# One block for the edge loop and the last stage of an edge-gated graph kernel, with the further passes ahead of both

## What is computed

```python
pre_u = einsum('bud,dk->buk', h, W1[:256]);  pre_v = einsum('bvd,dk->bvk', h, W1[256:])
S   = sigmoid(einsum('buvk,ko->buvo', relu(pre_u[:,:,None] + pre_v[:,None] + b1), W2)[...,0] + b2[0])
a_t = einsum('buv,bud->bvd', S * adj, h)
m_t = einsum('uv,bud->bvd', adj, h) * h
out = beta1*h + beta2*(a_t @ Wa + ba) + beta3*(m_t @ Wm + bm)
```

## Time and profile before

| | us |
|---|---|
| median of 3 runs | 3447.57 |
| lowest and highest | 3445.82, 3448.07 |
| the profiled execution, its own time | 3449.29 |
| its span, first to last instruction | 3447.2 |
| PE busy in the span | 3356.6 (97%) |
| DVE, ACT, POOL busy | 2841.7, 2342.5, 1836.9 |

### The profile page before, as it was taken

How to read it: one execution, slowest core, us unless ns; L and a number is a source line. 1 busy time by engine, 2 the same in 40 slices (tenths; PEclk the granted TensorE clock), 3 DMA queues, 4 the chain that set the end, 5 groups by cost and what they waited for, 6 DMA issues and landing times. The chain is left out here.

```text
span 3447.2 us, 56125 instructions
## 1 busy us (share of the span) xinstructions
PE 3356.6 (97%) x14230; PEld 2618.5 (76%) x14230; DVE 2841.7 (82%) x4857; ACT 2342.5 (68%) x14070; POOL 1836.9 (53%) x2379
## 2 busy tenths in 40 slices
PE   7999999999998999999999999999999999689999
PEld 5667667676666888778878888878878888578888
DVE  5566765766547999999999999999999999469897
ACT  1222121221116999899999999999999999688997
POOL 3221221221114667656666676666666665578886
PEclk9999999999999999999999999999999999899999
DMA  7876777767669656775675666666656647587775
GB/s 273 296 262 240 264 255 247 284 248 256 230 205 225 155 122 165 165 171 139 139 174 132 176 137 159 171 152 153 168 141 168 155 114 189 183 285 249 263 257 193
DMA packets 345402, 685.80 MB, mean 199 GB/s; under 512 B 38990, under 2 KB 252856, under 8 KB 323512
## 3 DMA queue, kind: packets, MB, share of 16 engines
q1 hardware_dynamic: 289088, 594.50, 59.6%
q0 software_dynamic: 21504, 53.31, 5.0%
q10 hardware_dynamic: 34480, 34.34, 2.9%
HBM read 444.01 MB, written 256.18 MB: 203 GB/s over the span
## 5 line engine op out<-in xcount | busy, mean ns | idle before, releaser
L1240 ACT ACTIVATE junk<-psum_a 128x128 f32<-128x128 f32 x6144 | 1611.5, 293 | 199.0 <-PE psum_a L1144 110.2
L1240 ACT ACTIVATION_READ_ACCUMULATOR junk<-psum_a 128x1 f32 x6144 | 1367.8, 224 | 0.0
L1185 DVE TENSOR_REDUCE group_sum<-psum_d 128x56 f32<-128x896 f32 x1024 | 1111.5, 1085 | 87.8 <-PE psum_d L1144 42.0
L1144 PE MATMUL psum_d<-v_t,pk 128*128 128x512 f32 x1920 | 754.6, 393 | 0.0
L1292 POOL DMA_INDIRECT sum_dram<-total,idx_all x512 | 506.9, 990 | 228.3 <-POOL total L1303 124.1
L996 POOL TENSOR_TENSOR own<-whole 128x256 f32<-128x256 f32 x128 | 126.0, 985 | 753.9 <-DVE own_mixed L789 420.3
L1143 PE MATMUL psum_d<-u_t,pk 128*128 128x512 f32 x1280 | 503.9, 394 | 5.8 <-issue 4.7
L689 PE MATMUL wide<-shared,h 128*128 128x512 f32 x1024 | 482.2, 593 | 0.0
L747 ACT COPY whole<-ring 128x256 f32<-128x256 f32 x128 | 47.7, 373 | 630.4 <-PE ring L661 630.4
L1144 PE MATMUL psum_a<-v_t,pk 128*128 128x512 f32 x1152 | 453.4, 394 | 0.0
L1604 ACT ACTIVATE masked<-masked,of_u,half_sign 128x128 f32<-128x128 f32 x1024 | 399.7, 480 | 61.7 <-POOL masked L1541 61.7
(11 more groups left out here) (225 smaller groups left out, 5532.8 us busy)
## 6 DMA issues: line engine op xcount, KB each, us to landing
rows_dram<-split SPq DMA_DIRECT2D x128, 512.0 KB, 3.2
sum_dram<-zero SPq DMA_DIRECT2D x128, 512.0 KB, 4.0
u_t<-rows_dram SPq DMA_DIRECT2D x64, 1024.0 KB
shared<-sum_dram SPq DMA_DIRECT2D x64, 1024.0 KB, 6.3
first_u<-rows_dram SPq DMA_DIRECT2D x62, 1024.0 KB
pk<-pick_dram SPq DMA_DIRECT2D x448, 128.0 KB
whole_dram<-whole SPq DMA_DIRECT2D x128, 256.0 KB, 3.4
pick_dram<-first_v SPq DMA_DIRECT2D x128, 256.0 KB, 3.0
```

The source lines that it names most:

```text
L1144: return nc.tensor.matmul(dst, pk[n % PKS][:, SLOTS + at:SLOTS + at + P], part(v_t[n % VG][:], b, LB), start=False, stop=True)
L1185: nc.vector.tensor_reduce(out_[:, :, 1:EG], in_[:, :, GW:LATE].rearrange("p b (g k) -> p b g k", k=GW), AX, ALU.add, apply_absolute_value= ...
L1240: last = nc.scalar.activation(junk[:, a % RING_A, k * LATE:(k + 1) * LATE], psum_a[a % RING_A][:, k * LATE:(k + 1) * LATE], ACT.Abs, accum ...
```

## The change

- `passes_i` is read into registers right behind the first stage, and the branch over the further passes stands there, ahead of the edge loop (before, both stood behind it). A semaphore `passes_made` says that DVE has written the number; SP also waits for all `rows_stored` there, since further passes would read those rows.
- Edge loop and last stage are one block: the functions `edges_sp`, `edges_pe` and so on, each followed by `last_sp`, `last_pe` and so on, on the same engine. The barrier, the reading of the register and the branch between them are gone. In their place PE waits for the last drained sums, and SP and POOL for all scatters.
- The POOL adds of tiles k = 0 and 1 are made inside the edge loop, one half each behind the scatters of cells n = 251 to 254.
- Their outputs `masked0` and `masked1` (`masked_ahead`) take the place of the second `hWa_ahead` tile in `shared`: only `hWa_all[0]` is loaded ahead, and `hWa_all[1]` is the first load of `last_sp`. The adj tiles of k = 0 and 1 are loaded ahead.
- DVE scales `of_u` behind cell 254 in place of behind cell 255.

Lines that only moved or were indented anew are left out; where one is shown for its place it has the old indentation.

```diff
@@ first stage: behind its last work, and behind the block
-                            link(nc.vector.tensor_copy(passes_i[:], most[:, 1:2]))
+                            nc.vector.tensor_copy(passes_i[:], most[:, 1:2]).then_inc(passes_made, 1)
...
+                    for i in range(RW):
+                        sp.wait_ge(rows_stored[i], 32 * ((B * NT - i + RW - 1) // RW))
+                    sp.wait_ge(passes_made, 1)
...
+            passes = nc.values_load(passes_i[0:1, 0:1], min_val=0, max_val=PASSES)
             nc.all_engine_barrier()
...
+        with nc.If(passes > 1):
...
-        hWa_ahead = [shared[:, i * ROW:(i + 1) * ROW].rearrange("p (b d) -> p b d", d=D) for i in range(RAW)]
+        hWa_ahead = shared[:, 0:ROW].rearrange("p (b d) -> p b d", d=D)
+        masked_ahead = [shared[:, ROW + i * P * B:ROW + (i + 1) * P * B].rearrange("p (b v) -> p b v", v=P) for i in range(RAW)]
@@ edge loop, SP at n == AHEAD
                             for t in range(RAW):
                                 sp.dma_start(raw[t], sum_uv[t * P:(t + 1) * P, 0:P, :]).then_inc(raw_loaded[t], 16)
-                                sp.dma_start(hWa_ahead[t], hWa_dram[:, t * P:(t + 1) * P, :].rearrange("b p d -> p b d")).then_inc(hWa_loaded[t], 16)
+                            sp.dma_start(adj_first[t][:], adj[t * P:(t + 1) * P, 0:P]).then_inc(adj_loaded[t], 16)
+                        sp.dma_start(hWa_ahead, hWa_dram[:, 0:P, :].rearrange("b p d -> p b d")).then_inc(hWa_loaded[0], 16)
@@ edge loop, POOL behind the scatters of cell n
+                    if n >= n_blk - 5 and n < n_blk - 1:
+                        k, m = divmod(n - (n_blk - 5), 2)
+                        some = slice(m * HV, (m + 1) * HV)
+                        pool.wait_ge(raw_loaded[k], 16)
+                        pool.wait_ge(of_v_loaded[m], 16)
+                        pool.wait_ge(left_d, LD * LEFT)
+                        pool.wait_ge(left_a, LA * LEFT)
+                        TT(masked_ahead[k][:, :, some].rearrange("p b v -> p v b"), raw[k][:, some, :], of_v[:, some, :],
+                           ALU.add).then_inc(raw_added, 1)
+                for i in range(RING_S):
+                    pool.wait_ge(scattered[i], 16 * TILES * ((n_blk - i + RING_S - 1) // RING_S))
@@ behind the edge loop
-            nc.all_engine_barrier()
-        passes = nc.values_load(passes_i[0:1, 0:1], min_val=0, max_val=PASSES)
-        with nc.If(passes > 1):
...
+            def last_pe(pe):
+                pe.wait_ge(drained_d, ND * n_blk)
+                pe.wait_ge(drained_a, NA * n_blk)
...
-                            if RAW <= k < NT:
+                        if 1 <= k < NT:
...
+                @block.gpsimd
+                def _(pool):
+                    edges_pool(pool)
+                    last_pool(pool)
```

More of the change, by code:

```diff
@@ L93, in gnn_edges_kernel @@
         of_v = sb("of_v", [P, P, B])
+        adj_first = [sb(f"adj_first{i}", [P, P]) for i in range(2)]
+        warm = sb("warm", [P, 1])
         shared = sb("shared", [P, 3 * ROW])
@@ L482, in gnn_edges_kernel @@
             at_made = sem("at_made")
+            passes_made = sem("passes_made")
             first_loaded = [sem(f"first_loaded{i}") for i in range(2)]
@@ L725, in _ @@
                                 index_left(left, NT - 1)
+                    pe.wait_ge(passes_made, 1)
                 @block.scalar
@@ L764, in _ @@
                             take_turned(b + 1)
+                    act.wait_ge(passes_made, 1)
                 @block.vector
@@ L1509, in step_done, with last_sp @@
                     eng.wait_ge(gate_used, (NT - 1) * vt + t + 1)
+            def last_sp(sp):
+                for vt in range(NT):
+                    for t in range(NT):
+                        k = vt * NT + t
+                        if t == 1 and vt:
+                            sp.wait_ge(raw_added, 2 * (k - RAW) + 1)
+                            load_of_v(sp, 2 * vt + 1, of_vs[(2 * vt + 1) % 3])
+                        if k >= RAW:
+                            sp.wait_ge(raw_added, 2 * (k - RAW + 1))
+                        if t == 3 and vt + 1 < NT:
+                            load_of_v(sp, 2 * vt + 2, of_vs[(2 * vt + 2) % 3])
+                        if k >= RAW:
+                            sp.dma_start(raw[k % RAW], sum_uv[t * P:(t + 1) * P, vt * P:(vt + 1) * P, :]).then_inc(raw_loaded[k % RAW], 16)
+                        if k >= 2:
+                            waits(sp, gate_masked, MASKS * (k - ADJ + 1))
+                            sp.dma_start(adj_b[k % ADJ][:], adj[t * P:(t + 1) * P, vt * P:(vt + 1) * P]).then_inc(adj_loaded[k % ADJ], 16)
+                        if 1 <= k < NT:
+                            sp.dma_start(hWa_all[t], hWa_dram[:, t * P:(t + 1) * P, :].rearrange("b p d -> p b d")).then_inc(hWa_loaded[t], 16)
@@ new lines, in last_pool @@
+            def last_pool(pool):
+                for vt in range(NT):
+                    for t in range(NT):
+                        k = vt * NT + t
+                        if k < RAW:
+                            continue
+                        pool.wait_ge(raw_loaded[k % RAW], 16 * (k // RAW + 1))
+                        step_done(pool, k - GM)
+                        for m in range(2):
+                            pool.wait_ge(of_v_loaded[m], 16 * (vt + 1))
+                            some = slice(m * HV, (m + 1) * HV)
+                            nc.gpsimd.tensor_tensor(masked[k % GM][:, :, some].rearrange("p b v -> p v b"), raw[k % RAW][:, some, :],
+                                                    of_vs[(2 * vt + m) % 3], ALU.add).then_inc(raw_added, 1)
@@ new lines, in last_pe @@
+            def last_pe(pe):
+                pe.wait_ge(drained_d, ND * n_blk)
+                pe.wait_ge(drained_a, NA * n_blk)
+                for vt in range(NT):
+                    for t in range(NT):
+                        k = vt * NT + t
+                        if vt == 0:
+                            pe.wait_ge(hWa_loaded[t], 16)
+                        for b in range(B):
+                            if b % HB == 0:
+                                pe.wait_ge(gate_masked, MASKS * k + b // HB + 1)
+                            if t == 0 and b % 2 == 0:
+                                waits(pe, z_ready, (vt - 1) * (B // 2) + b // 2 + 1)
+                            last = nc.tensor.matmul(z_psum[b // 2][:, (b % 2) * D:(b % 2 + 1) * D], masked[k % GM][:, b, :],
+                                                    hWa_all[t][:, b, :], start=(t == 0 and b % 2 == 0), stop=(t == NT - 1),
+                                                    skip_group_check=True)
+                            if t == NT - 1 and b % 2:
+                                last.then_inc(z_summed, 1)
+                        if t < NT - 1:
+                            last.then_inc(gate_used, 1)
```

668 lines of the change are left out of this document (312 added, 356 removed).

## The result

The changed kernel takes 3443.11 us (median of 20 runs, 3440.2 to 3444.97), the kernel before 3449.06 us in the same comparison (20 runs, 3445.82 to 3450.99). The ratio is 0.9983, 95% interval 0.9977 to 0.9988: 5.95 us less, just within the 0.2% that the prediction called no change. The forecast was 2.2 us less, 3445.4. The sign and both ranges held, the narrow one (3443 to 3450) by 0.1 us, which is luck.

A forecast was written before the change was run, and what follows sets the result against it. DMA was taken to bound the last stage until `raw` 8 lands, then PE for 389.7 us. Terms -9.0 (seam), +5.6 (load) and +1.2 (front) sum to -2.2 us: 3445.4, own range 3443 to 3450, wider range 3439 to 3453.

The forecast's parts named there:

- What bounds the stage: Last stage: DMA bounds 2975 to 3040 us, then PE for 389.7 us; PE's 27.81 us gap is off the path.
- The seam, -9.0: Between edge loop and last stage: SP's first large load issued at 2963.8 instead of 2972.8, 9.0 us earlier (bounds 10.0 and 4.1).
- The lag: POOL's last scatter ends later because four adds stand ahead of it: 4.2 us, plus 1.0 for the last cell.
- the 3.37 of the rival: POOL's adds in the edge loop take 3.37 us each instead of 2.40, giving a lag of 8.1 us.
- the term for DVE's multiplies: POOL's last edge-loop cell, beside DVE's first mask multiplies, takes 1.0 us longer, bounds 0 and 2.
- the 5 us of full exclusion: Two DVE multiplies hold POOL's last cell for at most some 5 us instead of 1.0; total then 3449.4.
- The load, +5.6: `hWa_all[1]` ahead of `raw` 2 costs the DMA-bound part 5.6 us (bounds 0 and 5.6); `raw` 8 lands 70.9 us behind first issue.
- less than 67 us: Sign of a wrong prediction: `raw` 8 landing less than 67 or more than 73 us behind the first large issue.
- The front, +1.2: Seam behind the first stage: register load and branch delay the edge loop by 1.2 us, at most 1.7, upper bound 5.6.
- cells 2 and 3 shifted by more than SP's loads are: Sign of a wrong prediction at the edge loop's opening: these cells move later by more than SP's loads do.
- the load is free: Rival: `hWa_all[1]` costs the DMA-bound part nothing, sum -7.8 us, 3439.8; chance 0.12.
- the slow side: Rival: POOL's lag of 8.1 us and SP stalling at the branch, +6.1 us, 3453.7; chance 0.18 for some slowdown.

The follow-up runs named there:

- the nine with the branch ahead: The changed kernel, its repeat and the follow-up kernels with register load and branch ahead of the edge loop; edge loop's end 1928.7 to 1930.8 us, mean 1929.7.

## Why the prediction was right, and where it was not

1. **What bounds the stage**: right. PE's closing 389.7 us are 389.4, 15.5 us from landing to PE stood to 0.1, and PE's gap of 27.81 us was worth nothing.
2. **The seam, -9.0**: right, -9.54. SP issues 1.26 us behind the last scatter's end (counted 1.4). The lag was put at 5.2 and measured 4.81. The adds took 2.37 to 2.44, the lower bound, and not the 3.37 of the rival; the term for DVE's multiplies was 1.0 and showed as one instruction, `two`, of 1.16 in place of 0.29, starting at 2960.11 while DVE multiplied. The scatter beside the next multiply was not held up (1.00 us), so the 5 us of full exclusion were never near. The first large issue was forecast for about 2965 (with the front) and came at 2966.24.
3. **The load, +5.6**: the step that failed is "it will land 70.9 us behind the new one". The load itself was sized well (4.2 taken out, 5.4 added). What failed is the 65.3 us carried over as if it belonged to the transfers. It belonged to the transfers at their addresses: 62.3 us at the new ones, so -3.0 for free. 62.3 + 4.2 = 66.5. The prediction had named less than 67 us as a sign that it was wrong, and that sign came.
4. **The front, +1.2**: mis-sized. It counted instructions up to SP's first issue (measured 1.1), and bounded the rest at 1.7 with the assumption that SP's issues behind it run as before. Mostly they don't (1.5 us more on the mean); the term is 2.3 on the mean, 2.98 in the profiled pair. PE began cell 1 3.25 us later and cell 2 3.18, SP's first load 1.54: the sign "cells 2 and 3 shifted by more than SP's loads are" came too.
5. **The sum**: -9.54 + 4.2 - 3.0 + 2.98 = -5.4, against -2.2. The two misses, -4.4 and +1.8, partly cancel. Without the addresses, which the prediction didn't know of, the sum would be -2.4; that this is so near -2.2 is luck as well, since three terms were off by -0.5, -1.4 and +1.8. Of the rivals, "the load is free" came nearer in size (-7.8) for a wrong reason; the slow side (POOL's lag with a stall at the branch) had a real mechanism in the wrong places: POOL did stall at a branch, but in *before*, and PE's stall of 3.44 us was covered (PE still waited 2.43 us ahead of cell 1).

So the 5.4 us in the traces are -14.35 for barrier, branch and wait at the seam, +2.98 for the branch in its new place, +4.8 for the adds ahead of the last scatters, +4.2 for a load that lost its cover, and -3.0 for an address that nobody chose.

## What to carry to other kernels

A stretch that DMA bounds has a rate, and the rate is a property of addresses too: when a change moves an allocation, don't carry GB/s over, look at where the destinations begin, and start large buffers on a multiple of 256 bytes, as every kernel with the higher rate here does. At a seam, ask for each piece of work that is moved ahead of the last dependency whether anything waits for it sooner; POOL's adds were moved ahead of what all waited for, and cost their own length beyond POOL's slack. Independent loads are what belongs there.

## What the runs showed of the hardware that I had not expected

- Equal DMA share, 7% fewer bytes: 367 to 372 GB/s with `shared` and `hWa_all` at 25,312 and on, 394 to 398 at 26,368 (or 25,344) and on; in the loads of `hWa_all` alone near 350 against 387.
- A branch over a long body stalls an engine behind it without a row of its own: POOL idle for 3.7 us behind a branch of 58 ns, while PE's branch shows its 4.36 and 3.44 us. SP's first two DMA issues of the edge loop took 2.04 us in the changed kernel (1.24 to 2.45 in the nine with the branch ahead) where 1.09 was before.
- POOL's small add waited for DVE: 1.16 us for one of 0.29. The multiply of DVE beside it, from which it was freed (timeline of DVE):

```profile
2959.79 1.32 DVE L1569 TENSOR_TENSOR shared<-shared,adj_first 128x1024 f32<-128x1024 f32 x1 [5.11 <-ACT shared L1611]
```

It ends at 2961.11, and POOL's at 2961.27. The Trainium skill (SBUF — State Buffer, "SBUF: two separate sides") has this lock between a DVE instruction with two inputs in SBUF and a GpSimd read; this row agrees.
- A scatter of POOL beside such a multiply is not held up: 1.00 us, as in before (POOL, then DVE):

```profile
2962.69 1.00 POOL L1440 DMA_INDIRECT sum_dram<-total,idx_all  x1 [0.77 <-POOL total L1451]
```

```profile
2962.80 1.23 DVE L1569 TENSOR_TENSOR shared<-shared,adj_first 128x1024 f32<-128x1024 f32 x1 [1.69 <-ACT shared L1611]
```

- The last scatter, 128 rows, takes 2.1 us to land with nothing beside it and 3.8 to 5.5 us with 4 to 6 MB of loads issued ahead of it.
